# Sparse attention with routed experts on one Trainium2 core: pacing GpSimd's key gathers and turning the keys later in the chunk

## The reference, cut to what matters

```python
h = _layernorm(x, axis=-1) * (1 + ca) + sa
q, k, v = (qkv[0], qkv[1], qkv[2])                      # h @ qkv_w.T + qkv_b
routing_scores = sigmoid(sigmoid(relu(h @ r_w1.T + r_b1) @ r_w2.T + r_b2))
attn = jnp.einsum('bhqd,bhkd->bhqk', q, k) / jnp.sqrt(D)
k_keep = max(1, int(tgt_len * 0.4))                     # 819
_, top_idx = jax.lax.top_k(rs_t, k_keep)                # per head
w = softmax(where(keep, attn, NEG_INF))
x = x + ga * einsum('bhqk,bhkd->bhqd', w, v)
h = _layernorm(x, axis=-1) * (1 + cb) + sb
x = x + gb * (one expert per token: relu(h @ fc)**2 @ proj)
```

## Time and profile before

| | before |
|---|---|
| median of 3 timed runs | 525.98 us (523.41 to 526.09) |
| profiled execution, span | 558.4 us |
| TensorE busy, matmuls | 451.8 us, 81% |
| VectorE busy | 396.4 us, 71% |
| ScalarE busy | 311.3 us, 56% |
| GpSimd busy | 217.7 us, 39% |

### The profile page before, as it was taken

One profiled execution on the slowest core, in us unless ns is written; L12 is line 12 of the kernel. 1 busy time (PEld: TensorE's weight loads), 2 busy tenths in 40 slices (PEclk: granted clock), 3 DMA queues, 4 the chain that ended last, 5 costly groups with the idle time before them and its releaser, 6 DMA issues.

```text
span 558.4 us, 9397 instructions
## 1 busy us (share of the span) xinstructions
PE 451.8 (81%) x3252; PEld 221.0 (40%) x3253; DVE 396.4 (71%) x1063; ACT 311.3 (56%) x457; POOL 217.7 (39%) x301
## 2 busy tenths in 40 slices
PE   4674754789999997998999899999999770769665
PEld 4341621223433432443434333333333270658564
DVE  8788864758986996787689668888889558134323
ACT  3435000357785785676578567778778740446333
POOL 3100576523414375266248425442003000655643
PEclk9878555569997999999799989999999955788878
DMA  7034300620100100100010010010000040211100
GB/s 230 0 126 118 82 6 6 217 90 4 32 2 6 33 3 5 30 6 6 3 32 3 6 32 2 6 33 2 2 2 0 22 133 0 76 41 42 44 17 12
DMA packets 20207, 21.11 MB, mean 38 GB/s; under 512 B 5740, under 2 KB 15792, under 8 KB 20160
## 3 DMA queue, kind: packets, MB, share of 16 engines
q1 hardware_dynamic: 14704, 16.12, 9.6%
q0 software_dynamic: 5168, 4.00, 3.9%
q10 hardware_dynamic: 288, 0.39, 0.2%
HBM read 14.41 MB, written 7.27 MB: 39 GB/s over the span
## 4 chain that ended last, share of the span: by engine, by line
PE 67%; DVE 16%; issue 7%; another core or an unknown queue 3%; DMA 2%; ACT 2%; POOL 1%; SPq 0%; POOLq 0%; DVEq 0%; ACTq 0%
PE OP L1501 17%; PE ST L1485 13%; PE ST L1461 6%; PE SC L1439 6%; PE SC L1437 6%; DVE tile_max L1067 5%; PE SC L1620 4%; PE ST L1631 3%; DVE PR L937 2%; PE OP L1509 2%; PE SC L1391 2%; DMA QS<-MT 2%; PE OP L1586 1%; PE SC L1441 1%
## 5 line engine op out<-in xcount | busy, mean ns | idle before, releaser
L1067 DVE TENSOR_REDUCE tile_max<-SC 128x1 f32<-128x410 f32 (+1 forms) x512 | 271.4, 577 | 74.9 <-PE SC L1437 49.2
L791 ACT ACTIVATE PR<-ST 128x1024 f32<-128x1024 f32 (+1 forms) x224 | 208.7, 962 | 62.4 <-PE ST L1485 57.0
L562 POOL DMA_INDIRECT G<-kv_dram,idx x104 | 106.8, 1027 | 169.0 <-ACT PR L791 108.8
L1485 PE MATMUL ST<-QS,KT 51*128 51x512 bf16 (+1 forms) x416 | 112.8, 403 | 3.6 <-DMA QS<-MT 2.7
L1501 PE MATMUL OP<-PR,VS 128*32 128x512 f32 x768 | 111.2, 653 | 0.4 <-ACT PR L791 0.4
L1437 PE MATMUL SC<-KT,QS 48*128 48x410 bf16 x256 | 80.6, 370 | 8.5 <-DVE tile_max L1067 4.5
L1485 PEld LDWEIGHTS ST<-QS,KT 51*128 51x128 bf16 (+1 forms) x416 | 30.2, 97 | 55.5 <-issue 39.3
L1439 PE MATMUL SC<-KT,QS 48*128 48x409 bf16 x128 | 47.3, 370 | 4.0 <-DVE tile_max L1067 1.1
L1441 PE MATMUL SC<-KT,QS 48*128 48x358 bf16 x128 | 43.4, 339 | 5.8 <-DVE tile_max L1067 3.7
L1620 PE MATMUL SC<-HT,PR 128*128 128x128 f32 x184 | 29.9, 316 | 18.3 <-issue 15.7
L686 POOL DMA_INDIRECT KV<-rows_dram,owner x23 | 24.3, 1054 | 50.5 <-DVE owner L1273 43.8
(11 more groups left out here) (257 smaller groups left out, 555.2 us busy)
## 6 DMA issues: line engine op xcount, KB each, us to landing
kv_dram<-KV SPq DMA_DIRECT2D x4, 512.0 KB, 2.9
WE<-in_w_fc SPq DMA_DIRECT2D x1, 2048.0 KB
WE<-in_w_proj SPq DMA_DIRECT2D x1, 2048.0 KB
G<-kv_dram,idx POOLq DMA_INDIRECT x104
q_parts_dram<-QP SPq DMA_DIRECT2D x3, 512.0 KB, 3.7
QS<-q_parts_dram SPq DMA_DIRECT2D x16, 96.0 KB
X<-in_x SPq DMA_DIRECT2D x4, 256.0 KB, 6.1
QS<-q_parts_dram SPq DMA_DIRECT2D x16, 64.0 KB
```

The source lines that it names most:

```text
L562: pool.indirect_dma_start(G[:, i % 2, slot_of(s), :], None, kv_dram, bass.IndirectOffsetOnAxis(ap=idx[:, i, s:s + 1].bitcast(U32), axis=0) ...
L791: nc.scalar.activation(PR[:, k, 0:cols], ST[:, (KSTEPS * n + k) % 2, 0:cols], ACT.Exp, scale=float(D) ** -0.5).then_inc(exp_done, 1)
L1067: v.tensor_reduce(tile_max[:, n % 2, at_col:at_col + 1], bank(RING_AT["unit", u])[:, 0:410 - f], AX.X, ALU.max).then_inc(s_reduced, 1)
L1485: last = mm(ST[:, at_step % 2, 512 * e:512 * e + 512], KT[rows, i % 2, P * tile:P * tile + P], QS[rows, i % 2, CHUNK * c:CHUNK * (c + 1)], ...
```

## The change

GpSimd's wait for its own weighting (`o_norm`) goes from `gathers`. The gathers of pairs 3 to 7 no longer stand behind the columns and the weighting: the columns' three operations go one by one behind the first three gathers, and the weighting behind the fifth. Their due times move from 1, 3, 5, ... 25 exponentials behind the start of chunk 4(i-2)+1 to 5, 6, 8, ... 27. `turn_k` and `copy_kt` move from step 2 of their chunk to step 5, behind `weigh_shared` on TensorE and behind the exponential of step 5 on ScalarE, and the ring's table with them (`TURN_AFTER`).

```diff
--- before.py
+++ after.py
@@ -51,8 +51,9 @@
 KSTEPS = 7
 RING = 3
 
-GATHER_FROM = [0, 0, 0] + [NQ * (i - 2) + 1 for i in range(3, NP)]
-TURN_AFTER = 7
+PACE = [0, 1, 3, 5, 7, 9, 11, 13, 15, 17, 19, 20, 22]
+GATHER_FROM = [0, 0, 0] + [KSTEPS * (NQ * (i - 2) + 1) + 5 for i in range(3, NP)]
+TURN_AFTER = 14
 
 AHEAD = 5
 LIST_BESIDE = {NQ * (i - 3) + 3: i for i in range(AHEAD, NP)}
@@ -555,10 +556,9 @@
                 pool.wait_ge(idx_ready, i + 1)
                 if i >= 2:
                     pool.wait_ge(v_ready, i)
-                    pool.wait_ge(o_norm, 2 * (i - 2))
                 for s in tiles:
                     if i >= 2:
-                        pool.wait_ge(exp_done, KSTEPS * GATHER_FROM[i] + 2 * s + 1)
+                        pool.wait_ge(exp_done, GATHER_FROM[i] + (PACE[s] if i >= 3 else 2 * s + 1))
                     pool.indirect_dma_start(
                         G[:, i % 2, slot_of(s), :], None, kv_dram,
                         bass.IndirectOffsetOnAxis(ap=idx[:, i, s:s + 1].bitcast(U32), axis=0),
@@ -627,45 +627,48 @@
             pool.wait_ge(prepared0, 2)
             prep_v(0)
             prep_v(1)
-            def columns(i):
+            def columns(i, step):
 
                 done = 3 * (i - AHEAD)
-                pool.wait_ge(idx_mm, i - AHEAD + 1)
-                pool.wait_ge(v_ready, i - 1)
                 by_code_of = B1[:, i % AHEAD].rearrange("p t e c -> p (t e) c")
                 by_tile = B1[:, i % AHEAD].rearrange("p t e c -> p t (e c)")
                 shape = [P, NT * 2, CODES]
-                nc.gpsimd.tensor_tensor(by_code_of, key_of[:, i, :, :].rearrange("p t (e a) -> p (t e) a", a=1)
-                                        .to_broadcast(shape),
-                                        cc("code").rearrange("p (h c) -> p h c", h=1).to_broadcast(shape),
-                                        ALU.subtract).then_inc(columns_late, 1)
-                pool.wait_ge(columns_late, done + 1)
-                nc.gpsimd.tensor_scalar(by_code_of, by_code_of, 0.0, None, ALU.is_equal).then_inc(columns_late, 1)
-                pool.wait_ge(columns_late, done + 2)
-                nc.gpsimd.tensor_tensor(by_tile, by_tile, token.rearrange("p (t c) -> p t c", c=1)
-                                        .to_broadcast([P, NT, 2 * CODES]), ALU.mult).then_inc(columns_late, 1)
+                if step == 0:
+                    pool.wait_ge(idx_mm, i - AHEAD + 1)
+                    pool.wait_ge(v_ready, i - 1)
+                    nc.gpsimd.tensor_tensor(by_code_of, key_of[:, i, :, :].rearrange("p t (e a) -> p (t e) a", a=1)
+                                            .to_broadcast(shape),
+                                            cc("code").rearrange("p (h c) -> p h c", h=1).to_broadcast(shape),
+                                            ALU.subtract).then_inc(columns_late, 1)
+                elif step == 1:
+                    pool.wait_ge(columns_late, done + 1)
+                    nc.gpsimd.tensor_scalar(by_code_of, by_code_of, 0.0, None, ALU.is_equal).then_inc(columns_late, 1)
+                else:
+                    pool.wait_ge(columns_late, done + 2)
+                    nc.gpsimd.tensor_tensor(by_tile, by_tile, token.rearrange("p (t c) -> p t c", c=1)
+                                            .to_broadcast([P, NT, 2 * CODES]), ALU.mult).then_inc(columns_late, 1)
 
             def index(i):
                 pool.wait_ge(rows_copied, i - AHEAD + 1)
                 pool.wait_ge(v_ready, i)
-                if i + 1 < NP:
-                    pool.wait_ge(columns_late, 3 * (i + 1 - AHEAD + 1))
+                pool.wait_ge(columns_late, 3 * (i - AHEAD + 1))
                 nc.gpsimd.tensor_tensor(rows16[:, :], rows16[:, :], row_add[:, STEPS * i:STEPS * (i + 1)], ALU.add)\
                     .then_inc(row_sum, 1)
                 pool.wait_ge(row_sum, i - AHEAD + 1)
                 nc.gpsimd.tensor_copy(idx[:, i, :], rows16[:, :]).then_inc(idx_ready, 1)
 
             for i in range(2, NP):
-                if AHEAD <= i + 1 < NP:
-                    columns(i + 1)
                 if i >= AHEAD:
                     index(i)
                     pool.wait_ge(idx_ready, i + 1)
-                elif i + 1 >= AHEAD:
-                    pool.wait_ge(columns_late, 3)
+                for s in range(3):
+                    gathers(i, range(s, s + 1))
+                    if AHEAD <= i + 1 < NP:
+                        columns(i + 1, s)
+                gathers(i, range(3, 5))
                 if i >= 3:
                     weighted(i - 3)
-                gathers(i)
+                gathers(i, range(5, STEPS))
                 prep(i)
                 prep_v(i)
             weighted(NP - 3)
@@ -798,8 +801,6 @@
                 if n >= 1:
                     copy_o(n - 1)
                 weights(n, 2, 3)
-                if n % NQ == 1 and n // NQ + 1 < NP:
-                    copy_kt(n // NQ + 1)
                 weights(n, 3, 2)
                 if n >= 1:
                     act.wait_ge(otr_done, n)
@@ -813,6 +814,8 @@
                     copy_rows(LIST_BESIDE[n - 1])
                 weights(n, 4, 3)
                 weights(n, 5, 4)
+                if n % NQ == 1 and n // NQ + 1 < NP:
+                    copy_kt(n // NQ + 1)
                 weights(n, 6, 4)
             copy_o(NCH - 1)
             copy_ot(NCH - 1)
@@ -1567,13 +1570,13 @@
                         if n >= 1:
                             weigh(n - 1, (5, 6))
                         unit()
-                    if k == 2 and n % NQ == 1 and n // NQ + 1 < NP:
-                        turn_k(n // NQ + 1)
                     if k == 4:
                         weigh(n, (0, 1), first=True)
                         unit()
                     if k == 5:
                         weigh_shared(n)
+                        if n % NQ == 1 and n // NQ + 1 < NP:
+                            turn_k(n // NQ + 1)
                 weigh(n, (2, 4))
                 unit()
                 assert not units
```

## The result

The changed kernel took 521.86 us (median of 20 runs, 516.38 to 523.93), the kernel before 524.38 us (median of 20 runs on the same chips). The ratio is 0.9953, with a 95% interval of 0.9931 to 0.9974: about half a per cent or 2.5 us less, which is small but clear of the scatter.

What follows compares the result with a forecast made beforehand. TensorE was taken to set the pace, with VectorE close behind. The terms -2.6 + 0 + 0 us took 525.98 us to 523.4 us, with a range of 515 to 528 us.

Steps and rivals of the forecast that it cites:

- Part 1: Turning keys at step 5 instead of step 2 costs 0.42 instead of 0.79 us in seven chunks: 2.6 us less.
- The narrow place: Step 6's exponential, pushed back by the key copy, meets its first reader in the next chunk with about 0.1 us spare.
- Rival 2: Key copy gets in the way of step 6's exponential on ScalarE: 3.9 us more, 529.8 us; chance 0.10.
- Part 2: Pacing GpSimd's gathers costs and gains nothing; keys are ready 1.8 us ahead of the later turn.
- Part 3: Columns' operations between gathers may hold up VectorE's subtractions: between -0.3 and +3 us, taken as 0.
- Rival 4: Columns' second operation falls on the subtractions in chunks 10, 14 and 18, about 1 us each: 526.4 us; chance 0.06.
- Rival 1: Stopped chunks are real and even pacing removes them: 508.0 us whole, 515.7 us half; chance 0.20.
- the 32.4 us: Excess of the profiled execution (558.4 us) over the timed median (525.98 us), taken as absent from timed runs.
- the stops: VectorE and ScalarE standing still without a releaser in chunks 6, 10, 14, 18, 22, 15.4 us above clean; no gain counted.
- Rival 3: The turning chunk's 0.37 us of idle time is VectorE's and appears elsewhere in the chunk: 526.0 us; chance 0.12.

Runs made afterwards that it cites:

- e1: The kernel before, unchanged, run for a second trace: 524.25 us, ratio 1.0016 to the kernel before.
- e9: The kernel before with one wait added, so GpSimd starts the columns only after VectorE has split the maxima: 524.74 us, ratio 1.0015.
- e3: The kernel after with the turn of the keys put back to step 2, gathers still paced: 554.77 us, ratio 1.0594 to the kernel before.
- e4: The kernel before with the turn at step 5 and all 13 gathers of pairs 3 to 7 in one run: 536.29 us, ratio 1.0255.
- e7: The kernel after with the weighting ahead of the gathers and the old due times, columns between: 521.93 us, ratio 0.9948 to the kernel before.
- e10: The kernel before with the turn at step 5 and the columns waiting for the split maxima, no pacing: 521.41 us, ratio 0.9941.
- e11: The kernel before with the turn at step 5, 13 gathers in one run and columns waiting for the split maxima: 523.00 us, ratio 0.9964.
- e2: The kernel before with only the turn of the keys and their copy moved to step 5: 525.29 us, ratio 1.0033.

## Why the prediction was right, and where it was right for another reason

- **The forecast.** 2.6 us less was forecast, 2.5 us less measured, and the ratio forecast by it, 0.995, is the one measured.
- **Part 1, the turn.** Its mechanism was right and is shown. The turning chunk came to 9.98 us where 9.90 was worked out, so the term is 7 x 0.30 = 2.1 us and not 2.6. The narrow place held: the key copy began 0.04 us behind the end of step 5's exponential (198.45), step 6's exponential began at 199.30, 8.61 us into the chunk where 8.66 was computed, and the chunk's end moved back by 0.50 us, 0.08 more than the 0.42 us of TensorE's work in the sum; 0.06 of that is TensorE's busy time. Rival 2 did not happen.
- **An unforeseen side of it.** In two traces with the turn at step 2 and no wait for GpSimd (e1, which is one of the longer executions of before, and e9), 7 of 14 turning chunks also had a clock fall, 1.3 to 1.5 us each; in the first trace of before none of chunks 5 to 25 had one; in the ten traces with the turn at step 5, 1 of 70. Clean chunks fall now and then too: 10 of 176 in the eleven traces other than the first of before, e3 and e4, with TensorE idle for 0.11 us. None of this was a gain that the medians show: the median granted clock of after and before is the same (0.868 and 0.869), so in the kernel after the half speed lies elsewhere, above all in the list chunks (chunk 15 above, at 0.69).
- **Part 2, the gathers.** Taken at nothing, and right: e7 with the old times, e10 without pacing and e11 with all in one run all reach the figure of after or come within 0.3% of it. The preparation ended 4.96 us into the chunk against 5.3 at the latest. What the part left out is what happens if the turn is not moved: e3, 31 us, most of it TensorE's wait for the keys and the clock behind it, the rest holds by the columns.
- **Part 3, the columns.** Taken at 0 on the strength of one row: a hold of 1.2 us that cost chunk 9 only 0.08 us. The term is right, because in the kernel after the columns' two-input operations meet no subtraction; the one-input one of 2.5 us does, as the prediction feared (201.79 to 204.29 over the subtraction at 203.87, in the last section), and costs nothing. The reasoning is not. A hold ahead of TensorE's turn of the maxima came with up to 5 us (e4), where it stopped TensorE and the clock fell behind it, and with 1.5 us where the clock stayed (e3, chunk 10). In chunk 9 of before the hold fell on the second subtraction and TensorE had the turn's work beside it; whether that is why it was cheap there was not tried. Rival 4's mechanism is real, but not with the operation that it named, and its price of 1 us a chunk lies between the 0.08 and 0.45 us of the mild cases (before, e2) and the 5 us of e4. By the runs the change would have been worth nothing without this part: the turn alone gives 1.0033, with the columns made to wait 0.9941, and these intervals don't meet. The sum has nothing for that, so that it came so near is in part luck: it took a kernel with holds for its start, priced the turn at 2.6 us, and the turn by itself brought nothing that the runs can tell.
- **The parts don't add up.** Turn alone +0.3%, wait alone +0.2%, both -0.6%. Each single figure is within about its interval of nothing, but the sum is not within that of both. That an early turn and a hold each leave TensorE idle, and that the clock falls then, would make them alternatives of one loss; that reading is argued from single traces, the falls in clean chunks speak against so simple a rule, and it stays open.
- **Rival 1 and the 32.4 us.** What failed here is the reading that the 32.4 us, and with them the stops, belong to the profile and not to the timed runs ("they were the profiler's"). Every timed run for which a span is on record has it 1.8 to 1.9 us below its time (520.4 and 522.17 us for the profiled run of after), so profiling costs nothing of that size. The stops belonged to one uncommon execution. Leaving them out of the sum was right for that reason, and not for the one given. What caused them isn't known: e4 and e1 show that runs of gathers alone don't.
- **Rival 3** did not happen: the idle time of the turning chunk went from 0.48 to 0.13 us and no neighbouring chunk grew.

## What to carry to other kernels

When a helper engine's work is moved, look first at what it comes to lie over on an engine that it can hold up, and only then at due times: here the place of one operation of 1.7 us on GpSimd came with a half per cent gained or two and a half lost. What an edit saves on the engine that sets the pace can vanish if another engine's operation lies badly beside it. And a profile of one execution should be held against the spread of the timed runs before its oddest feature is explained.

## What the runs showed of the hardware

- A two-input operation on GpSimd (L638, 1.69 us) held a two-input subtraction on VectorE until its very end when they met: 1.38 us in the earlier trace rows, 1.67, 1.67 and 1.66 us in e4. In e3 two subtractions that began 0.3 and 0.6 us ahead of such an operation (L648, 1.70 us), beside a gather, were also held to its end (2.02 and 2.33 us); why is open, as a gather alone left dozens of them at 0.15 to 0.19 us.
- A one-input operation on GpSimd held it only near its own start. The short conversion L587 did so to its end, in chunk 17 of the kernel after; the columns' second operation, of 2.5 us, left the subtraction of chunk 10 at its ordinary 0.15 us in the middle of it (each time POOL, then DVE):

```profile
280.63 0.36 POOL L587 CAST KS<-KR 128x208 bf16<-128x208 f32 x1
...
280.73 0.28 DVE L1084 TENSOR_TENSOR NM<-NM 128x8 f32<-128x8 f32 x1
...
201.79 2.50 POOL L645 TENSOR_SCALAR B<-B 128x896 f16<-128x896 f16 x1
...
203.87 0.15 DVE L1084 TENSOR_TENSOR NM<-NM 128x8 f32<-128x8 f32 x1
```

  A subtraction that came 0.35 us behind the start of that long operation took 0.60 us (e4, e2 above, and chunks 13 and 17 of before), so it was free again 0.95 us behind the start; one that came 0.90 us behind it took 0.16 us (chunk 13 of e1). The Trainium skill, "SBUF — State Buffer", section "SBUF: two separate sides", has the hold last for the whole of any GpSimd operation that reads SBUF; the measurements bear that out for the two-input operations and the short conversion, and not for the long one-input operation.
- An idle time of TensorE cost several times itself where the clock fell behind it. In e3 a wait of 2.37 us made chunk 9 longer by 4.7 us; in e4 one of 1.43 us made chunk 8 longer by 5.0 us, with a mean granted clock of 0.68, that is partly at 1.2 GHz instead of 2.4. It did not always fall: a hold that left TensorE idle for 1.32 us in chunk 10 of e3 cost 1.5 us at a clock of 1.00. And it fell without such an idle time, in clean chunks (10.8 us at 0.84, in e1).
- Between runs of one kernel the spread follows that clock: the kernel before ran from 519 to 530 us beside the experiments, with a mean granted clock of 0.88 in the fastest of them and 0.85 in the slowest.
